# Filler products of 256 constant columns before the tail steps of a four-layer decoder on TensorE

## Time and profile before

| | us |
|---|---|
| median of 3 runs | 801.65 |
| the three runs | 802.94, 801.65, 794.07 |
| the profiled execution's own time | 793.75 |
| its span, first to last instruction | 791.6 |
| around the span | 2.2 |
| TensorE busy (matmul) | 673.8 |
| VectorE, ScalarE, GpSimd busy | 549.0, 443.8, 438.1 |
| mean granted TensorE clock, share of full speed | 0.871 |

### The profile page before, as it was taken

The page is one execution under the profiler, slowest core; times in us unless marked ns, Lnnn a source line. Parts: engine busy times, 40 slices in busy tenths (PEclk is TensorE's granted clock), DMA queues, the critical chain, the costliest instruction groups (busy, mean ns, idle before and its releaser), DMA issues.

```text
span 791.6 us, 23001 instructions
## 1 busy us (share of the span) xinstructions
PE 673.8 (85%) x8884; PEld 504.0 (64%) x8884; DVE 549.0 (69%) x1479; ACT 443.8 (56%) x1092; POOL 438.1 (55%) x606
## 2 busy tenths in 40 slices
PE   5988886889999987999986989878997889958990
PEld 2665653577777874777544767638955567746990
DVE  4867858977888754888458998443557689853654
ACT  2225634678888753877524776345727557622671
POOL 2248837976777622354226896344675558554550
PEclk8558958999999995999996999688999879957995
DMA  9049000000000000000009300004115481004212
GB/s 307 20 158 212 3 2 0 2 2 2 2 2 2 2 2 1 2 4 3 2 2 202 120 2 4 2 28 101 45 64 176 146 250 47 4 29 101 64 37 87
DMA packets 50793, 44.30 MB, mean 56 GB/s; under 512 B 15904, under 2 KB 41376, under 8 KB 50176
## 3 DMA queue, kind: packets, MB, share of 16 engines
q1 hardware_dynamic: 48448, 38.24, 17.6%
q0 software_dynamic: 2240, 4.60, 1.7%
HBM read 29.95 MB, written 12.88 MB: 54 GB/s over the span
## 4 chain that ended last, share of the span: by engine, by line
PE 57%; DVE 16%; issue 8%; POOL 8%; ACT 4%; DMA 4%; SPq 1%; DVEq 0%; ACTq 0%; POOLq 0%
PE bank L937 5%; PE bank L916 5%; PE bank L924 4%; PE bank L1003 3%; PE bank L1119 3%; PE bank L1194 3%; PE bank L1201 2%; DVE sm L1687 2%; PE bank L1028 2%; PE bank L1069 2%; PE bank L1053 2%; DVE mx L1689 2%; PE bank L948 2%; PE bank L831 2%; PE bank L1076 2%
## 5 line engine op out<-in xcount | busy, mean ns | idle before, releaser
L2107 POOL TENSOR_TENSOR sm<-sm,mx 128x512 f32<-128x512 f32 x80 | 84.2, 1053 | 37.7 <-DVE mx L1689 37.4
L1292 ACT COPY pT<-bank 128x512 f32<-128x512 f32 x112 | 65.4, 584 | 44.6 <-PE bank L924 43.6
L1288 ACT ACTIVATE pr<-sm 128x512 f32<-128x512 f32 x112 | 70.7, 634 | 26.1 <-POOL sm L2107 24.5
L924 PE MATMUL bank<-W,pr 128*128 128x128 f32 x448 | 75.0, 293 | 6.6 <-ACT pT L1292 4.4
L2074 POOL TENSOR_SCALAR veps<-mv 128x1 f32<-128x1 f32 x104 | 23.3, 224 | 100.7 <-DVE mv L1623 100.5
L916 PE MATMUL bank<-pairs,Q 64*64 64x256 f32 x896 | 67.6, 420 | 5.8 <-DVE sm L1681 2.9
L2102 POOL TENSOR_TENSOR pairs<-KS,quad 128x512 f32<-128x512 f32 x48 | 50.8, 1059 | 37.7 <-ACT KS L1271 37.5
L924 PEld LDWEIGHTS bank<-W,pr 128*128 128x128 f32 x448 | 53.1, 148 | 19.1 <-issue 11.1
L2075 POOL TENSOR_TENSOR rstd<-veps,W 128x1 f32<-128x1 f32 x104 | 59.3, 570 | 8.7
L937 PEld LDWEIGHTS bank<-VX,pT 64*64 64x64 f32 x3072 | 53.3, 143 | 9.4 <-issue 4.8
L937 PE MATMUL bank<-VX,pT 64*64 64x9 f32 (+1 forms) x3072 | 57.2, 205 | 1.2 <-ACT pT L1292 0.7
(11 more groups left out here) (399 smaller groups left out, 1864.5 us busy)
## 6 DMA issues: line engine op xcount, KB each, us to landing
big<-gup SPq DMA_DIRECT2D x4, 1024.0 KB, 9.8
rel_scratch<-G SPq DMA_DIRECT2D x16, 256.0 KB, 2.9
W<-small SPq DMA_DIRECT2D x1, 3206.5 KB, 12.2
big<-early SPq DMA_DIRECT2D x2, 1557.0 KB, 8.4
slots_x<-zero SPq DMA_DIRECT2D x2, 1472.0 KB, 24.5
big<-down SPq DMA_DIRECT2D x8, 256.0 KB, 8.6
QM<-rel_scratch SPq DMA_DIRECT2D x16, 128.0 KB, 3.0
PM<-rel_scratch SPq DMA_DIRECT2D x16, 128.0 KB, 2.8
```

Of the source, the lines that this page charges most:

```text
L924: last = pe.transpose(tile(ps, p), pr[:, u % 2, 4 * h + p, :, :].rearrange("p b k -> p (b k)"), ident)
L1288: act.activation(pr[:, u % 2, 4 * h:4 * h + 4, :, :].rearrange("p g b k -> p (g b k)"), sm[:, 2 * (u % 2) + h, :], ACT.Exp, scale=a["scale ...
L1292: act.copy(pT[:, u % 2, 4 * h:4 * h + 4, :], bank[BK[f"tu{h}"]][:, :].rearrange("p (h n) -> p h n", h=4)).then_inc(pt_ready, 1)
L2107: tt(v, v, bc(mx[:, slot, :], [P, 8, S], 2), ALU.subtract).then_inc(pcentered, 1)
```

## The change

In front of every `fo`, `y` and `x` of the last tiles of `x0`, `x2` (tiles 6 and 7) and `x3` (5 to 7), of every `y` and `x` of `gelu` from tile 1 on, and of every `in`, `y` and `x` of `ema`, TensorE calls `keep_busy` once with 256 columns, on the bank that the step is about to claim. In `first_ffn` it does so in front of every step after the last `sc`. In `top2_ffn` it multiplies three times 512 columns into bank 7 in front of the wait for VectorE's choice.

```diff
+THIN = {(name, step): t for name, t, steps in (("x0", 6, ("fo", "y", "x")), ("gelu", 1, ("y", "x")), ("ema", 0, ("in", "y", "x")),
+                                               ("x2", 6, ("fo", "y", "x")), ("x3", 5, ("fo", "y", "x"))) for step in steps}
...
-            def keep_busy(b, n):
+            def keep_busy(b, n, wide=512):
 
                 pe.wait_ge(*hold[b])
                 for _ in range(n):
-                    mm(bank[b][:, :], ident, plenty, start=True, stop=True)
+                    mm(bank[b][:, 0:wide], ident, plenty[:, 0:wide], start=True, stop=True)
...
                 for step, name, u, t, s_, h in planned[part]["pe"]:
+                    if (name, step) in THIN and t >= THIN[name, step] and BK[step] in hold:
+                        keep_busy(BK[step], 1, 256)
                     a = att.get(name)
...
             def first_ffn():
-                for step, l, t, n in local["pe"]:
+                last_scores = local["pe"].index(("sc", 1, MT - 1, 2 * MT - 1))
+                for i, (step, l, t, n) in enumerate(local["pe"]):
                     h = HT[:, 2 * t:2 * t + 2, :].rearrange("p b k -> p (b k)")
                     b_ = LOCAL_BANK[step]
+                    if i > last_scores:
+                        keep_busy(b_[0], 1, 256)
...
             def top2_ffn():
                 logits("e3.r", NE3, range(MT - 1, MT))
+                keep_busy(7, 3)
                 pe.wait_ge(one_ready, 4)
```

## The result

The changed kernel takes 818.25 us (median of four runs, 810.08 to 831.72); the kernel before, run beside it, takes 800.0 (four runs, 794.07 to 802.94). The ratio is 1.0255, with a 95% interval of 1.0173 to 1.0338: slower by 14 to 27 us, where 13.4 was forecast. The profiled execution took 819.22 us.

What follows compares the result with a forecast made beforehand. TensorE, busy in 85% of the span with a falling clock, was taken to bound the kernel. Terms 14.2 - 3.8 + 5.5 + 0.9 - 3.4 = +13.4 us on 798.1 gave 811.5 us, range 801 to 822.

Steps and rivals of the forecast that it cites:

- The total, +13.4: Whole kernel: all terms together make it 13.4 us slower, 811.5 us, with a range of 801 to 822.
- End of first_ffn, +14.2: Steps behind first_ffn's last scores: 34 fillers cost 13.5 us where TensorE is full, the other 14 cost 0.7.
- Head of a1, -3.8: Start of a1: fillers between first_ffn's last turns may keep the clock up, saving 3.8 us of at most 6.8.
- The +17.2: Whole kernel: the sum if fillers do not suffice to hold the clock and the head of a1 saves nothing.
- Second turn of gelu, +5.5: Gelu's second tile: the filler waits for bank 2 and holds four wide products back, delaying the turn by 5.5 us.
- Rival 3: Gelu: the wait for bank 2 costs nothing, since VectorE could have released it earlier; +8.4, or 806.5; chance 0.08.
- Rest of gelu and the moving average, +0.9: Gelu's rest and ema: full clock saves 1.6 us, then ten ema fillers cost 2.5 where TensorE is nearly full.
- Tails, -3.4: Tails of x0 (+0.6), x2 (-1.7), x3 (-1.4) and top2 (-0.9): gains from full clock, less what fillers cost.
- the prediction's own sign: Tails: the forecast counts as wrong if the clock there stays at 0.50.
- the 0.15 us for each hand-over: Tails of x2 and x3: at full clock the chains keep about 0.15 us in each of five hand-overs, -0.7.
- The first, that first_ffn absorbs its fillers: End of first_ffn: other engines set the pace, fillers cost about 1 us, a1 gains 6.8; -2.8, or 795.3; chance 0.10.
- The second, that the clock falls all the same: Whole kernel: fillers are paid at 0.88 us and a1 gains 0; +29.2, or 827; chance 0.12.

Runs made afterwards that it cites:

- The order in gelu: The changed kernel without the one filler ahead of gelu's second turn, so the four wide products stand first in the queue again; 813.14 us, ratio to before 1.0165.

## Why the prediction was right, point by point

- **The total, +13.4.** The time lies in the range, but above the figure: 14 to 27 us were measured. The terms that cost, 14.2, 5.5 and 0.9, add up to 20.6, near the 20 of the ratio; the two gains set against them, -3.8 and -3.4, did not show in the time. The range held because it left room for both gains to fail, not because those two terms were right.
- **End of first_ffn, +14.2.** Right in place, mechanism and size. The 34 fillers were put at 13.5 between 8.5 and 14.6, and they cost 13.48: 12.93, and 0.55 for the first. Of their 34 x 0.44 = 15.0 us only 1.5 fell into idle time. The reading that decided it, that no wait stands in front of these steps, held; the record of 0.4 us of idleness was too small, as the text allowed. The last 14 were put at 0.7 between 0 and 2.6 and cost 1.84: the second group of `dn` products comes 1.1 us later already (304.27 - 296.63 against 294.94 - 288.43).
- **Head of a1, -3.8.** The step that failed is "with fillers between its last turns the clock may stay up", taken as lasting through the head. The clock did stay at 1.00 through all the turns, and then fell to 0.50 at 311.99, 0.18 us into a1's first projection. From first projection to third scores the three kernels with all fillers of first_ffn at 256 columns gave -0.5, -0.5 and -2.75, the one with 128 columns -0.6, the one with the last 14 alone -4.19, the one without `fy` 0, and six with none there 0 to -1.55. The size was right for a clock that holds; that it holds was not given. The Trainium skill, "TensorE: Matmul & The Clock Gate", Part 4, on transposes, by which turns do not engage the full clock, is neither borne out nor refuted here: the clock stayed at 1.00 through turns with fillers between them (297.50 to 312.00) and fell behind them, and no run has the turns apart from the fillers. The +17.2 that the prediction gave by it came nearer to the measured time than its own +13.4.
- **Second turn of gelu, +5.5.** Right: +6.18 in the changed kernel, +5.79 and +5.74 in two others, and 0 without that one filler. The row of fillers begins 0.40 us after the start of VectorE's sum (420.13 against 419.73) and not before. The stretch that stood between 3.96 and 7.9 took 426.32 - 420.13 = 6.19, at a mean clock of 0.64. Rival 3, by which the wait costs nothing, is out.
- **Rest of gelu and the moving average, +0.9.** +1.5 in the changed kernel, +2.1 alone: inside the bounds. Cut at 438.5 of the kernel before, where ema and x2 begin to interleave, the changed kernel gains 1.6 ahead of it and loses 3.1 behind, where -1.6 and +2.5 were forecast. Alone, with some fillers paid at half clock, the two are +0.1 and +2.0: the gain ahead of 438.5 is not there in every execution either.
- **Tails, -3.4.** The weakest step. x2 was to gain 1.7; it does gain 2.4 where the clock holds, but its fillers change nothing in the whole time that can be told from scatter. x3 was to gain 1.4; it loses 2.9 to 3.5 in three profiles, near the end of +3 given for it, and gains 2.2 in the fourth. The step that failed is "at full clock some 5 us of dense work halve in each", for it takes a clock that stays up: in the changed kernel it is at 0.61 and 0.70 in the two tails, and in the three losing profiles of x3 it falls within 0.6 us of the start of the first filler, which comes behind 0.73 us of idleness and the logits. By the prediction's own sign, a clock that stays at 0.50 in the tails, this part comes close to being wrong. No run shows the 0.15 us for each hand-over by itself. The three products of top2 are hidden, as forecast: they end before VectorE's choice (0.65 us idle stay of 3.33), and the first rank takes 0.43 in place of 0.69.
- **The rivals.** The first, that first_ffn absorbs its fillers, is refuted by the dense steps. The second, that the clock falls all the same, came true in the head of a1 and, in most profiles, in x3, not in first_ffn's turns.

What stays open: the parts measured alone add up to 3.8% (1.9, 0.59, 0.26, 0.74, 0.32), the whole to 2.55 with an interval up to 3.4. Five intervals of 0.3 to 0.6 each leave the sum about 1% of play, so that the two may well agree. The three products of top2 were not run alone. The 1.7 us gained between the head of a1 and gelu appear in all six kernels with fillers at the end of first_ffn, but also in one without (that of gelu and the moving average, -1.6); in each of these the clock no longer falls for a moment behind 384 to 390, as it does before and in the other five. What holds it up there was not isolated.

## What to carry to other kernels

Filler on an in-order engine costs its full length wherever the engine's queue has no wait, and a busy share below 100% doesn't prove one: look in the timeline for steps that have a wait in front of them, and put fillers only there. Even there it was not free: the last 14 steps of first_ffn lost 1.9 of their 6.2 us of filler. A filler must write to a bank that is already free, since on a bank that another engine still reads it waits, holds the whole queue behind it and turns a free 4 us of filler into late work. Of a clock that filler is to hold up, count no gain from one profile, since the same steps with the same fillers kept it in one execution and lost it in another, and weigh the gain against a measurement's scatter: here 4.2 us in one profile were not visible in the median.

## What was not expected of the hardware

- The same instructions, with the same fillers ahead, were granted 1.00 in one kernel and 0.65 on average in another. The last 14 steps of first_ffn and the head of a1 are identical in the kernel with the last 14 fillers (head 12.33 us) and in the changed one (327.80 - 311.81 = 15.99); only what ran ahead of them differs, and when they began. Even that need not differ: "The order in gelu" is the same program as the changed kernel up to gelu, and its clock fell 7.2 us after the start of a1's first projection and not 0.18 us after it, so that its head gained 2.75 us and not 0.5.
- The price of a filler is that of its columns: 34 of 256 columns 13.48 us, of 128 columns 6.51 (6.19 and 0.32 for the first). A matmul of float32 with 128 columns that is recorded with 0.27 to 0.30 us occupies TensorE for about 0.11 a pass: eight such passes take 1.05 us, and (1.05 - 0.27)/7 = 0.11.
- In VectorE's timeline the 5.63 us in front of the sum at 426.68 are marked as issue, that is, as waiting for nothing that the profile shows; TensorE's timeline shows that the turn whose result it reads ran only at 426.32. Where a long gap is marked so, the engine that writes its input tells the reason.
